# Flamingo gated block on one core: x of the query projections loaded by columns and normalised by spread rows

## The reference

```python
x = x + tanh(g_xattn[0]) * xattn(layernorm(x), ctx, ctx, adj, mask, Wq, bq, Wk, bk, Wv, bv, Wo, bo)
x = x + tanh(g_ffn[0]) * ffn(layernorm(x), ...)

def layernorm(x):                       # per token, over 512 features, eps 1e-5
    return (x - mean(x)) / sqrt(var(x) + eps)

def xattn(query, key, value, ...):      # 16 heads of 32
    Q = query @ Wq.T + bq ; K = key @ Wk.T + bk ; V = value @ Wv.T + bv
    scores = Q @ K.T / sqrt(32) + adj ; scores = where(mask == 0, -inf, scores)
    return softmax(scores) @ V @ Wo.T + bo
```

## Time and profile before

| | us |
|---|---|
| median of 3 runs (lowest, highest) | 1719.68 (1719.57, 1719.79) |
| the profiled execution, its own time | 1719.05 |
| its span | 1717.2 |
| PE busy in the span | 1693.4 (99%) |
| DVE, ACT, POOL busy | 1455.7, 1268.0, 662.6 |
| projections, from PE's first product to its last | 6.7 to 285.4 |

### The profile page before, as it was taken

How to read it: one execution, slowest core, us unless ns; L and a number is a source line. 1 busy time by engine, 2 the same in 40 slices (tenths; PEclk the granted TensorE clock), 3 DMA queues, 4 the chain that set the end, 5 groups by cost and what they waited for, 6 DMA issues and landing times. The chain is left out here.

```text
span 1717.2 us, 34352 instructions
## 1 busy us (share of the span) xinstructions
PE 1693.4 (99%) x12456; PEld 1296.1 (75%) x12456; DVE 1455.7 (85%) x2586; ACT 1268.0 (74%) x2241; POOL 662.6 (39%) x598
## 2 busy tenths in 40 slices
PE   9999999999999999999999999999999999999996
PEld 7888888777777777777777777777786685775863
DVE  7554554999999999999999999999778978969978
ACT  4222323999999999999999999999765476466556
POOL 3432341423378542586532785464323010100100
PEclk9999999999999999999999999999999999999998
DMA  8778675866367675378673676766515313412301
GB/s 281 276 248 286 228 272 160 191 176 146 114 171 192 129 170 122 111 215 173 128 171 92 180 189 130 152 136 152 159 57 160 90 50 98 139 50 52 112 25 50
DMA packets 162105, 258.92 MB, mean 151 GB/s; under 512 B 25616, under 2 KB 78096, under 8 KB 161952
## 3 DMA queue, kind: packets, MB, share of 16 engines
q1 hardware_dynamic: 110416, 158.84, 29.3%
q0 software_dynamic: 50960, 97.01, 24.8%
q10 hardware_dynamic: 576, 1.05, 0.2%
HBM read 168.47 MB, written 84.18 MB: 147 GB/s over the span
## 5 line engine op out<-in xcount | busy, mean ns | idle before, releaser
L1024 DVE CUSTOM_DVE_ANT_0 a_neg<-a_sc_ps,am 128x1024 f32<-128x1024 f32 x512 | 621.7, 1214 | 1.5 <-PE a_sc_ps L856 1.3
L964 ACT ACTIVATE a_prob<-a_neg,a_row_min 128x1024 f32<-128x1024 f32 x512 | 585.7, 1144 | 14.1 <-DVE a_row_min L1024 7.8
L870 PEld LDWEIGHTS a_tr_ps<-ident,a_prob 128*128 128x128 f32 x4096 | 461.1, 140 | 89.1 <-issue 53.4
L870 PE MATMUL a_tr_ps<-ident,a_prob 128*128 128x128 f32 x4096 | 519.8, 274 | 0.9 <-ACT a_probT L942 0.9
L999 DVE COPY a_probT<-a_tr_ps 128x512 f32<-128x512 f32 x512 | 350.6, 685 | 37.0 <-PE a_tr_ps L870 35.4
L942 ACT ACTIVATE a_probT<-a_tr_ps 128x512 f32<-128x512 f32 x512 | 303.8, 594 | 35.7 <-PE a_tr_ps L870 16.1
L752 POOL DMA_DIRECT2D a_q_st<-q_parts x144 | 79.6, 559 | 164.7 <-PE a_sc_ps L856 129.0
L856 PE MATMUL a_sc_ps<-k_first,a_q_st 96*128 96x512 f32 x384 | 126.3, 427 | 0.0
L856 PE MATMUL a_sc_ps<-a_k_st,a_q_st 96*128 96x512 f32 x384 | 125.9, 426 | 0.0
L890 PE MATMUL a_o_ps<-a_probT,a_v 128*32 128x256 f32 x2048 | 123.6, 382 | 0.6 <-ACT a_o L953 0.6
L890 PE MATMUL a_o_ps<-a_probT,v_first 128*32 128x256 f32 x2048 | 123.8, 382 | 0.0
(11 more groups left out here) (236 smaller groups left out, 3326.4 us busy)
## 6 DMA issues: line engine op xcount, KB each, us to landing
a_q_st<-q_parts POOLq DMA_DIRECT2D x144, 128.0 KB, 4.1
k_first<-k_parts POOLq DMA_DIRECT2D x24, 512.0 KB, 7.5
a_k_st<-k_parts POOLq DMA_DIRECT2D x24, 512.0 KB, 8.3
a_m_raw<-mask SPq DMA_DIRECT2D x24, 512.0 KB, 5.1
a_adj_raw<-adj SPq DMA_DIRECT2D x24, 512.0 KB, 6.2
k_parts<-p_out_hi SPq DMA_DIRECT2D x32, 256.0 KB, 5.3
k_parts<-p_out_lo SPq DMA_DIRECT2D x32, 256.0 KB, 6.4
v_all<-p_v_out SPq DMA_DIRECT2D x8, 1024.0 KB, 4.4
```

Of the source, the lines that this page charges most:

```text
L870: last = pe.transpose(tr_ps[:, bank(u, half), j * P:(j + 1) * P], prob[:, r % NPROB, t * P:(t + 1) * P], ident[:])
L964: act.activation(prob[:, r % NPROB, :], neg[:, r % 2, :], ACT.Exp, scale=-1.0, bias=row_min[:, r % 2:r % 2 + 1], accum_out=row_sum[:, r // ...
L1024: dve.tensor_tensor_reduce(out=neg[:, r % 2, :], in0=sc_ps[:, r % 2, :], in1=am[:, 2 * qb + qt, :], scale=-1.0, scalar=3.4e38, op0=ALU.add ...
```

## The change

x is given a second time, transposed on the host for each chunk (`xT`, features on rows), as the context already is. Chunk 0 is made as before. From chunk 1 on:

- PE makes no transposes. POOL loads the columns of x into the buffer of `xn` (now `x_cols`), once the low parts of the chunk before are made. x is loaded by rows too, for the statistics.
- POOL also copies the means beside the inverse deviations (`norm_cols`), stores both to DRAM as two rows of 512 (`stat_rows`), waits for that, and loads them into all 128 partitions (`norm_rows`). All of it stands between `inverse_std(c)` and `mask_tile(c)`.
- DVE subtracts the mean row and multiplies by the deviation row, feature tile by feature tile (`centre`, `scale`), between the low parts of K. `norm_apply` is gone, and `norm_stats(c + 1)` moves ahead of the reads of V (not in chunk 0, where it stays behind them).
- POOL's load of the next x by rows waits for the statistics of the chunk before and no longer for its normalisation.
- `mask_tile` waits for mask and adj together ahead of its first instruction.
- The chunk loops of PE, ACT, DVE and SP are written out.

```diff
             def inverse_std(c):
-                held_wait(pool, mv_ready, c + 1, pool_passed)
+                wait(pool, mv_ready, c + 1)
                 pool.tensor_scalar(var_eps[:], mv[:, :, 1], EPS, 1.0, ALU.add, ALU.mult).then_inc(var_ready, 1)
-                pool.wait_ge(var_ready, c + 1)
-                pool.tensor_tensor(rstd[:], var_eps[:], minus_half[:], ALU.pow).then_inc(rstd_ready, 1)
+                pool.tensor_scalar(mean, mv[:, :, 0], 1.0, 0.0, ALU.mult, ALU.add).then_inc(var_ready, 1)
+                pool.wait_ge(var_ready, 2 * c + 2)
+                pool.tensor_tensor(rstd, var_eps[:], minus_half[:], ALU.pow).then_inc(rstd_ready, 1)
...
+                pool.wait_ge(am_loaded, 32 * (t + 1))
                 pool.tensor_scalar(mask_stage, mask_stage.bitcast(I32), 0.0, -BIG, ALU.is_equal, ALU.mult).then_inc(big_ready, 1)
                 pool.wait_ge(big_ready, t + 1)
-                pool.wait_ge(adj_loaded, 16 * (t + 1))
...
+            def spread_norm(c):
+
+                pool.wait_ge(rstd_ready, c + 1)
+                with nc.allow_non_contiguous_dma(reason="columns become two rows"):
+                    pool.dma_start(stat_rows[c].rearrange("k (t p) -> p k t", p=P), norm_cols[:]).then_inc(norm_cols_stored, 16)
+                wait(pool, scaled, ET * (c - 1))
+                pool.wait_ge(norm_cols_stored, 16 * c)
+                pool.dma_start(norm_rows, stat_rows[c].partition_broadcast(P)).then_inc(norm_rows_loaded, 16)
+
             inverse_std(0)
             for c in range(1, NCH):
                 if c == 4:
                     first_group()
-                pool.wait_ge(xn_ready, c)
+                if c == 1:
+                    pool.wait_ge(xn_ready, 1)
+                else:
+                    pool.wait_ge(stats_ready, c)
                 pool.dma_start(x_raw[:], x[ds(c * CH, CH), :].rearrange("(t p) e -> p t e", p=P)).then_inc(x_loaded, 16)
                 pool.wait_ge(c_lo_ready, ET * c)
                 pool.dma_start(c_raw[:], ctxT[ds(c, 1)].rearrange("a (t p) s -> p (a t) s", p=P)).then_inc(c_loaded, 16)
                 if c == 1:
                     pool.wait_ge(w_lo_ready, 2 * ET)
                     mask_tile(0)
+                pool.wait_ge(xT_lo_ready, ET * c)
+                pool.dma_start(x_cols[:], xT[c].rearrange("(t p) s -> p t s", p=P)).then_inc(xT_loaded, 16)
                 inverse_std(c)
+                spread_norm(c)
                 mask_tile(c)
...
-                pe.wait_ge(xn_ready, c + 1)
-                for t in range(ET):
-                    for s in range(TT):
-                        last = pe.transpose(x_t[:, t, s * P:(s + 1) * P], xn[:, s, t * P:(t + 1) * P], ident[:])
-                    last.then_inc(xT_ready, 1)
                 if first:
+                    pe.wait_ge(xn_ready, 1)
+                    for t in range(ET):
+                        for s in range(TT):
+                            last = pe.transpose(x_t[:, t, s * P:(s + 1) * P], xn[:, s, t * P:(t + 1) * P], ident[:])
+                        last.then_inc(xT_ready, 1)
...
                 for t in range(ET):
-                    act.wait_ge(xT_ready, 4 * c + t + 1)
-                    act.activation(xT_hi[:, t, :], x_t[:, t, :], ACT.Copy).then_inc(xT_hi_ready, 1)
+                    if c == 0:
+                        act.wait_ge(xT_ready, t + 1)
+                        source = x_t
+                    else:
+                        act.wait_ge(scaled, ET * (c - 1) + t + 1)
+                        source = x_cols
+                    act.activation(xT_hi[:, t, :], source[:, t, :], ACT.Copy).then_inc(xT_hi_ready, 1)
...
+            def centre(c, t):
+                if t == 0:
+                    dve.wait_ge(xT_loaded, 16 * c)
+                    dve.wait_ge(norm_rows_loaded, 16 * c)
+                dve.tensor_tensor(x_cols[:, t, :], x_cols[:, t, :], norm_rows[:, 0, :], ALU.subtract).then_inc(centred, 1)
+
+            def scale(c, t):
+                dve.wait_ge(centred, ET * (c - 1) + t + 1)
+                dve.tensor_tensor(x_cols[:, t, :], x_cols[:, t, :], norm_rows[:, 1, :], ALU.mult).then_inc(scaled, 1)
...
+                    if normalised:
+                        centre(c, m)
+                        if m:
+                            scale(c, m - 1)
...
-                low_parts(c, 0, 0, bias_k)
-                if isinstance(c, int) and c == 0:
+                low_parts(c, 0, 0, bias_k, c > 0)
+                if c:
+                    scale(c, ET - 1)
+                if c == 0:
                     split_weight(2)
...
+                if c and more:
+                    norm_stats(c + 1)
                 wait(dve, v_stored, 16 * c)
                 for m in range(4):
                     dve.wait_ge(acc_ready, NACC * c + 4 + m + 1)
                     dve.tensor_tensor(v_out[:, m, :], acc[:, m, :], bv_rows[:], ALU.add).then_inc(acc_read, 1)
+                if c == 0:
+                    norm_stats(1)
                 if more:
-                    norm_stats(c + 1)
                     split_context(c + 1)
-                    norm_apply(c + 1)
                 low_parts(c, 8, 4, bias_q)
```

More of the change, by code:

```diff
@@ L52, in wait @@
     eng.wait_ge(sem, value)
[L55 to L60, removed]
 class Placer:
@@ L166, in three_pass, with project_phase @@
     return pe.matmul(acc, w_hi, r_lo, start=False, stop=last)
-def project_phase(nc, x, ctxT, WqT, bq, WkT, bk, WvT, bv, adj, mask, q_parts, k_parts, v_all, ident, am, k_first, q_first, v_first, stored, v_stored, small, g_xattn, g_ffn):
+def project_phase(nc, x, xT, stat_rows, ctxT, WqT, bq, WkT, bk, WvT, bv, adj, mask, q_parts, k_parts, v_all, ident, am, k_first, q_first, v_first, stored, v_stored, small, g_xattn, g_ffn):
     with ExitStack() as ctx:
@@ L199, in project_phase @@
         var_eps = sb("p_var_eps", [P, TT])
-        rstd = sb("p_rstd", [P, TT])
         minus_half = sb("p_minus_half", [P, TT])
+        norm_cols = sb("p_norm_cols", [P, 2, TT])
+        mean, rstd = norm_cols[:, 0], norm_cols[:, 1]
         acc = ctx.enter_context(nc.psum_tensor("p_acc", [P, 4, CH], F32))
         x_t = ctx.enter_context(nc.psum_tensor("p_x_t", [P, ET, CH], F32))
-        w_loaded = [sem(f"p_w_loaded{n}") for n in range(3)]
+        w_loaded = {n: sem(f"p_w_loaded{n}") for n in (1, 2)}
         b_loaded = sem("p_b_loaded")
@@ L319, in store_parts @@
                     sp.dma_start(tile(1), out_lo[:, m, :].bitcast(F32)).then_inc(stored[m], 16)
-            with sp.Fori(0, NCH) as c:
+            for c in range(NCH):
                 store_parts(c, k_parts, 0, 0)
@@ L384, in _ @@
             chunk(0, True)
-            with pe.Fori(1, NCH) as c:
+            for c in range(1, NCH):
                 chunk(c, False)
@@ L430, in _ @@
             chunk(0, True)
-            with act.Fori(1, NCH - 1) as c:
+            for c in range(1, NCH - 1):
                 chunk(c, True)
@@ L449, in norm_stats @@
                 last.then_inc(stats_ready, 1)
-                held_wait(dve, stats_ready, c + 1, dve_passed)
+                wait(dve, stats_ready, c + 1)
                 for s in range(TT):
@@ L453, in norm_stats, with norm_apply_rows @@
                 last.then_inc(mv_ready, 1)
[L455 to L458, removed]
+            def norm_apply_rows():
+                dve.wait_ge(rstd_ready, 1)
+                dve.wait_ge(mv_ready, 1)
                 for s in range(TT):
@@ L477, in _ @@
             norm_stats(0)
-            norm_apply(0)
+            norm_apply_rows()
             dve.wait_ge(b_loaded, 48)
@@ L496, in chunk @@
                     dve.wait_ge(xT_hi_ready, 4 * c + t + 1)
-                    dve.tensor_tensor(xT_lo[:, t, :], x_t[:, t, :], xT_hi[:, t, :].bitcast(F32), ALU.subtract).then_inc(xT_lo_ready, 1)
-                if isinstance(c, int) and c == 0:
+                    dve.tensor_tensor(xT_lo[:, t, :], (x_cols if c else x_t)[:, t, :], xT_hi[:, t, :].bitcast(F32), ALU.subtract).then_inc(xT_lo_ready, 1)
+                if c == 0:
                     dve.wait_ge(w_lo_ready, 3 * ET)
+                if c and more:
+                    norm_stats(c + 1)
                 wait(dve, v_stored, 16 * c)
@@ L503, in chunk @@
                     dve.tensor_tensor(v_out[:, m, :], acc[:, m, :], bv_rows[:], ALU.add).then_inc(acc_read, 1)
+                if c == 0:
+                    norm_stats(1)
                 if more:
-                    norm_stats(c + 1)
                     split_context(c + 1)
-                    norm_apply(c + 1)
                 low_parts(c, 8, 4, bias_q)
             chunk(0, True)
-            with dve.Fori(1, NCH - 1) as c:
+            for c in range(1, NCH - 1):
                 chunk(c, True)
@@ L1952, in gated_block @@
                             sem("weighted_loaded"), sem("weighted_step"), sem("weighted_stored"))
[L1953 removed]
```

(1 more changed line is left out.)

34 lines of the change are left out of this document (17 added, 17 removed).

## The result

The changed kernel took **1782.55 us** (median of 4 runs, 1781.99 to 1783.63) beside 1719.62 of the kernel before on the same chip: a ratio of **1.0365**, 95% interval 1.0353 to 1.0378. It is slower by 63 us, where 1717.7 was forecast with a range that ended at 1728. What follows first finds the 63 us in the trace.

What follows compares the result with a forecast made beforehand. PE, busy 99% of the span, was taken as the bound. -13.1 (transposes and one wait) + 4.9 + 4.8 (stalls) + 1.4 (clock) = -2.0 on 1719.05, so 1717.05, or 1717.7 as a median; range 1708 to 1728.

Steps and rivals of the forecast that it cites:

- Transposes, -12.6: PE in the projections: dropping the sixteen transposes saves 1.80 us in each of seven chunks, -12.6 in all.
- The 0.5 ahead of K0 of chunk 1: PE's wait for the low part of Q0, held behind `norm_apply` on DVE, goes: -0.5 us.
- The store, 3.0: In POOL's round, the store of 1024 four-byte elements was taken to land in 3.0 us, between 2.2 and 6.2.
- rival 2: Slow small store makes POOL's round the bound, from a store of about 5.6 us: +8 middle, +14 far end; chance 0.20.
- adj, 6.2 from its issue: In POOL's round, adj lands 4.9 us after issue, plus 1.3 for the 0.5 MB of rows ahead of it.
- Wrong altogether if PE waited in K or V, for `centre` behind late rows: Sign against the whole forecast: PE waiting in the K or V products because `centre` stands behind late rows; no size.
- Chunk 1, 4.9 (3 to 8): x of chunk 2 lands at +23.2 from K0 of chunk 1, wanted at +18.1: PE waits 4.9 us, 3 to 8.
- chunk 3, 4.8 (2 to 8): x of chunk 4, issued behind `first_group`, lands at +22.9 of chunk 3: PE waits 4.8 us, 2 to 8.
- The clock, 0.7 a stall: PE at half clock after each of the two stalls costs 0 to 2.7 us; 0.7 each taken, 1.4 in all.
- Rival 3: The two forecast stalls, but the clock falls after both, 2.7 us each: +2, 1721.7 us; chance 0.15.
- DVE ahead of V: `norm_stats` ahead of DVE's reads of V is the new point of danger: 1.3 us left, nil with x at +18.1.
- The locked port at 0: `centre` and `scale` on DVE and POOL's table instruction shut each other out: cost 0, at worst 1 us a chunk.

Runs made afterwards that it cites:

- e15: Changed kernel with four neighbouring tokens per partition, so the store has 256 pieces of 16 bytes, x's row load following: 1730.54 us, ratio 1.0057.
- e11: Kernel before plus, in each chunk, a load of 1024 four-byte pieces from DRAM into SBUF that nobody waits for: 1721.52 us.
- e14: Kernel before plus 1024 four-byte writes a chunk that nobody waits for, each 64 bytes from the next in DRAM: 1721.95 us.
- e4: Kernel before plus the same store of 1024 four-byte pieces in each chunk, constant data, not waited for until the phase's end: 1736.39 us, ratio 1.0095.
- e3: Changed kernel with the store as 128 pieces of 32 bytes, rows in another order than the tokens: 1728.41 us, ratio 1.0054.
- e12: Changed kernel with only `norm_stats` put back behind the reads of V in every chunk: 1780.33 us, ratio 1.0345.
- e9: Changed kernel, statistics turned by one PE transpose, stored as 512-byte rows; x loaded early; SP loads rows, context and columns: 1716.52 us, ratio 0.9975.

## Why the prediction was wrong, by its own steps

- **Transposes, -12.6: right.** e15's steady chunks of 32.64 against 34.44 give 1.80 each. The loops cost nothing there either. The 0.5 ahead of K0 of chunk 1 went as well: no wait stands there in the changed kernel.
- **The store, 3.0: the step that failed.** It measured 12.5, 13.2 until the next issue, and made POOL's round 42.0 where 32.64 was the bound. The row chosen as the nearest, 2.2 for 512 four-byte elements, was a *load*. e11 confirms it for loads (1024 in 2.9), and e14 even for writes that lie apart (3.4); but the store of the change writes neighbours. That no row of before shows such a store was said in rival 2 and then not carried into the bound: the upper end, 6.2, was a load too.
- **"The DMA engines stood idle at this place": true and beside the point.** It was given as the reason for the low end. In the changed kernel SP issues the V store 0.4 us behind the small one (84.61), and it took 11.6 instead of 4.4; e4 shows such delays with nobody waiting, and there the store takes 10.8 all the same.
- **adj, 6.2 from its issue: mis-sized too.** It took 10.0 in the round shown. Only about 1 us of that hangs on the slow store, since e3, where the store lands in 2.4, still has 8.7 for it. With the rest of the sum as forecast, this term alone would not have brought the round over 32.64; the store alone does (28.2 + 10.2 = 38.4).
- **Rival 2, right in mechanism, wrong in size.** POOL's round became the bound and every chunk stalled. Its deciding point for the store, 5.6, was passed twice over. Its far end, +14, fell short of +63, since chunks 2 and 4 to 6 lost 8 to 11 each and not 0.6. The round of 42.0 against 32.64 says 9.4 a chunk; priced so, the rival reads: six chunks of 9.4, ten more in each of chunks 1 and 3, less 12.6, which is +64. The chance of 0.20 was too low for the one edit whose price had no row.
- **"Wrong altogether if PE waited in K or V, for `centre` behind late rows": this came too**, once: PE stood 7.5 ahead of V1 of chunk 1 until 66.20, when DVE had waited 15.4 for the rows.
- **Chunk 1, 4.9 (3 to 8), and chunk 3, 4.8 (2 to 8): right places, too small.** e15 has 8.6 and 9.15, beyond both upper ends. (The terms of chunk 1 add up to 23.2 - 18.1 = 5.1, not 4.9.) The rule behind them held: x landed at 149.03, K0 of chunk 3 at 121.57, so +27.5 where +18.1 is wanted, 9.4, and PE waited 9.15. Off was POOL's place: it came to `first_group` at +10.7 (132.22) and not at +5.2, of which adj (9.2 for 6.2, issue at 116.49 to the table at 125.65) is the largest part and the store (4.8 for 3.0, issue to issue) the next.
- **The clock, 0.7 a stall: mis-sized.** 16.4 over seven gaps is 2.3 each; e15, counted in the same way, gives 10.1 + 12.6 - 17.7 = 5.0 over the stalls of two chunks. Rival 3's price of 2.7 was near. The Trainium skill (TensorE: Matmul & The Clock Gate, Part 1) says an idle PE falls to 1.2 GHz and returns only under load; the gaps here agree, with 0.50 to 0.61 in the 4 us behind each of the seven. I had taken 0.7 by leaning on one mild row, and the rule should have had the weight.
- **DVE ahead of V: a real place, no cause.** e12 costs as much without it.
- **The rule on small pieces** of the Trainium skill (DMA: Bandwidth & Descriptors, Specifications: transfers under 512 B are read-modify-written) pointed at the right edit. The runs narrow it: 4-byte pieces 64 bytes apart are as small and land in 3.4.
- **The locked port at 0:** nothing in the runs contradicts it; e15's steady chunks keep 32.64. It was not tried by itself.

Had the store been of e15's kind, the forecast of 1717.7 would still have been 12.8 low: (8.55 - 4.9) + (9.15 - 4.8) = 8.0 from the two stalls, 5.0 - 1.4 = 3.6 from the clock. The rest, 1.2, is not traced; 0.7 of it may be the chip, where the kernel before took 1720.34.

Open: why small writes to one stretch hold each other up, and why they hold up transfers of other queues, is not shown; only that they do, and when not.

## What to carry to other kernels

Price a store by a row of a store of the same pattern; if the profile has none, the edit has no upper bound, and the likeliest case must not rest on it. When an engine both waits for transfers and issues the next ones, write its round as a sum and compare it with the period of the bound engine: here the sum stood at 28.2 against 32.64, so any 4.5 us more would turn it, and one link of it had no price. Statistics that must change from a column to rows are better turned on the chip first (one 128x128 instruction, 0.16 a chunk), and the first steps of a changed pipeline left in the old way: with the loads moved off the engine that waits, that made a loss of 63 us a gain of 8.

## What the hardware showed unexpectedly

- 4 KB written as 1024 four-byte neighbours: 12.5 us (10.8 with less beside it); 512 of 8 bytes 7.0; 256 of 16 bytes 4.1; 128 of 32 bytes 2.4. Between 1024 and 256 that is close to 11 ns for each piece. The same 1024 pieces 64 bytes apart 3.4, 512 bytes apart 3.5; as loads 2.9.
- Such a store stops the others: 6 GB/s in 4 us of all 16 engines, Q stores of 256 KB at 10.8 for 2.9, from either queue.
- PE came back at half its clock (0.50 to 0.61 in the 4 us behind) after the gaps of 3.8 us and more that were looked at, at a cost of 1.8 to 3.8 us each. After gaps of 1.0 and 1.05 (e15, e9) the granted clock stayed at 1.00.
